# A two-layer cross-attention kernel: in the first layer's step, both halves of the weighted-value product stand together, the preparation follows them, and the second pair of search products comes last

## The chip, the cores and the metric

The kernel runs on one core of a Trainium2 chip. The metric is the device time of one execution in microseconds (us), the median of several runs. The core's engines run side by side, each through its own list of instructions in order, and wait for each other by semaphores: TensorE (PE in the profile; PEld is its weight load), VectorE (DVE), ScalarE (ACT), GpSimd (POOL) and SyncE (SP, which only issues DMAs). "Product" below means a matmul on TensorE.

## The reference

Two layers work on x (32 batches, 56 tokens, 128 channels) with a context of 1500 rows per batch. Each layer is a cross-attention and then a mixture of 8 experts. The attentions are

```python
# layer 0: 32 query-key heads of 4 channels, 16 value heads of 8; two softmaxes, their difference, an RMS norm
q, k, v = layernorm(x) @ Wq.T, ctx @ Wk.T, ctx @ Wv.T
a1 = softmax(q1 * hd**-0.5 @ k1.T) @ v;  a2 = softmax(q2 * hd**-0.5 @ k2.T) @ v
x = x + tanh(g) * (rms_norm(a1 - lam * a2) * subln_w * (1 - LAMBDA_INIT)) @ Wp.T + ...
# layer 1: 16 heads of 8 channels, a mask over the context
x = x + tanh(g) * (softmax(where(mask, -big, q @ k.T / sqrt(8))) @ v) @ Wo.T + ...
```

The change is in the attention of both layers; it matters in layer 0, which is the first half of the time.

## The kernel before

`attend` (one function for both layers) goes over the 32 batches, and in each over 12 key tiles of 125 keys: 384 *steps* a layer. The maximum of each query's scores is not found online: a *search* computes the scores of the next batch beforehand, in 48 *pieces* (112 queries by 500 keys, layer 0), four in each step, and VectorE takes the maximum of each piece. The pieces come in two pairs; the two products of a pair use different rows of TensorE. In this text **A0, A1** is the first pair of a step (`searched(n, t, 0)`) and **B0, B1** the second (`searched(n, t, 1)`). Layer 1 has only two pieces in a step, so it has no B pair.

In a step of layer 0, TensorE computes

- the *scores* of the tile (L850, two banks `score_ps`), from which ScalarE makes the exponentials `probs` (L943, two instructions);
- the pieces (L829), which VectorE reduces (L1001);
- the *weighted-value product* of the tile before (L866, fp32, `probs` times values into `acc_ps`), in two halves, `weigh(n, t - 1, 0)` and `weigh(n, t - 1, 1)`, four products each that use different columns of TensorE;
- mostly one *preparation*: a piece of work for another batch that is laid on a step by the table `where`. V is a third of the values (L803), T a third of the transposed context (L790), K a third of the keys (L798), F a transpose of the finished output (L813), A the transpose of the normalised output (L817), and M the transpose of the negated maxima (L808), which VectorE splits into two fp16 rows (L974, L976). All others are taken out of PSUM ("drained") by ScalarE.

Pieces and preparations share three PSUM banks, `spare_ps`, `max_ps0` and `max_ps1`, in strict rotation over the list `order`: whoever is at place k of that list waits until the one at place k - 3 has been drained. Before the change the places of a full step are A0 A1 B0 B1 and the preparation. So B0 waits for the preparation of the step before, B1 for A0, the preparation for A1, and the next step's A0 and A1 for B0 and B1. This is the wait:

```python
            def wait_for_room(user):

                k = place_of[user]
                if k >= len(rooms):
                    pe.wait_ge(*drained(order[k - len(rooms)]))
```

The keys of a batch go a long way: K on TensorE, ScalarE copies them out, GpSimd splits them into two fp16 parts (L720, L722), SyncE stores them to HBM (L618) and loads them into the rows of `kstack` (L628), three batches ahead. The first piece of a batch (A0 of step 7) waits for that.

Of the kernel before, what the change touches and what calls it, by code (L numbers as in the profile page):

```python
# [90 lines left out]
def at_least(eng, sem, value):  # L91

    if isinstance(value, int) and value <= 0:
        return
    eng.wait_ge(sem, value)


def build(nc, a, out):

    ctx = ExitStack()  # L100
    with ctx:
# [128 lines left out]
        feed_forward(T, 0)  # L230
        normalise(T, "norm1", 1)
        attend(T, L1)
        normalise(T, "norm1f", None, projected=1)
        feed_forward(T, 1)
# [218 lines left out]
def attend(T, L):  # L453
# [63 lines left out]

    if L is L0:
        where = {("V", 0): (0, 1), ("F", 0): (1, 1), ("F", 1): (2, 1), ("V", 1): (3, 1), ("T", 0): (4, 1), ("V", 2): (5, 1),
                 ("K", 0): (6, 1), ("M", 0): (7, 0), ("T", 1): (7, 1), ("K", 1): (8, 1), ("T", 2): (9, 1), ("K", 2): (10, 1),  # L520
                 ("A", 0): (11, 1)}
        keyed = [("T", 0), ("K", 0), ("T", 1), ("K", 1), ("T", 2), ("K", 2)]
    else:
        where = {("V", 0): (0, 1), ("F", 0): (1, 1), ("V", 1): (2, 1), ("F", 1): (3, 1), ("V", 2): (4, 1), ("K", 0): (5, 1),
                 ("K", 1): (6, 1), ("M", 0): (7, 0), ("K", 2): (8, 1), ("A", 0): (10, 1)}
        keyed = [("K", i) for i in range(NTHIRD)]
    valued = [("V", i) for i in range(NTHIRD)]
    per_step = L.pieces // NKT
# [14 lines left out]
    def at_step(n, t, side):  # L543

        return [(kind, n + LEAD[kind], i) for (kind, i), place in where.items()
                if place == (t, side) and 0 <= n + LEAD[kind] < B]

    def searched(n, t, k):


        if 2 * k >= per_step:
            return []
        d, place = (1, early + t * per_step) if t < NKT - AHEAD else (2, (t - NKT + AHEAD) * per_step)
        return [("P", n + d, place + 2 * k + r) for r in range(2)] if n + d < B else []

    order = [("P", 0, p) for p in range(L.pieces)] + [("M", 0, 0)] + [("P", 1, p) for p in range(early)]
    for n in range(B):
        for t in range(NKT):
            order += searched(n, t, 0) + at_step(n, t, 0) + searched(n, t, 1) + at_step(n, t, 1)
    order += [(kind, B - 1, i) for kind, i in turnaround]  # L560
    rooms = [spare_ps[:, :], max_ps[0][:, :], max_ps[1][:, :]]
    place_of = {user: k for k, user in enumerate(order)}
# [2 lines left out]
    def room(user):  # L565

        if user in place_of:
            return rooms[place_of[user] % len(rooms)]
        return first_banks[first_preps.index(user) % len(first_banks)]
# [9 lines left out]
    def piece(p):  # L579

        r, third, c, i = p % 2, p // 2 % NTHIRD, p // (2 * NTHIRD) % PAIRS, p // (2 * NTHIRD * PAIRS)
        return r, third, c, i, (i * 2 + r) * PAIRS + c

    with nc.Block() as block:
# [188 lines left out]
        def _(pe):  # L773
# [5 lines that stand above are left out]
# [40 lines left out]
            def search(pair):  # L819

                for _, n, p in pair:
                    if p == 0:
                        pe.wait_ge(s_ks[n % SLOTS], K_INC * (n // SLOTS + 1))
                        pe.wait_ge(s_qs, n + 1)
                for _, n, p in pair:
                    r, third, c, i, _ = piece(p)
                    rows = slice(HALF * r, HALF * r + KROWS)
                    wait_for_room(("P", n, p))
                    nc.tensor.matmul(room(("P", n, p))[0:PIECE, 0:TK], qstack[n % SLOTS][rows, c, PIECE * i:PIECE * (i + 1)],  # L829
                                     kstack[n % SLOTS][rows, c, TK * third:TK * third + TK],  # L830
                                     start=True, stop=True, skip_group_check=True).then_inc(s_piece, 1)
# [54 lines left out]
            for n in range(B):  # L886
                for t in range(NKT):
                    for h in range(H):
                        scores(n, t, h)
                    search(searched(n, t, 0))  # L890
                    for user in at_step(n, t, 0):
                        use(user)
                    for i in range(2):
                        if t:
                            weigh(n, t - 1, i)
                        elif n:
                            weigh(n - 1, LAST, i)
                        if i == 0:
                            search(searched(n, t, 1))
                    for user in at_step(n, t, 1):  # L900
                        use(user)
            for i in range(2):
                weigh(B - 1, LAST, i)
# [4 lines left out]
        @block.scalar  # L908
        def _(act):
            def drain(user):  # L910
                kind, n, i = user
                if kind == "M":
                    return
                spare_ps = room(user)
                act.wait_ge(s_ready, spare_count[user] + 1)
                if kind == "T":
                    if i == 0:
                        at_least(act, s_cst, 16 * n)
                    nc.scalar.activation(ctxT[0][:, TK * i:TK * i + TK], spare_ps[:, 0:TK], ACT.Copy).then_inc(s_ctxT, 1)
                if kind == "K":  # L920
                    at_least(act, s_kl, NTHIRD * (n - 1) + i + 1)
                    key = key_f[:, TK * i:TK * i + TK]
                    if L.masked:
                        nc.scalar.activation(key, spare_ps[:, 0:TK], ACT.Identity, bias=small["bk1"][:, :]).then_inc(s_kf, 1)
                    else:
                        nc.scalar.activation(key, spare_ps[:, 0:TK], ACT.Copy).then_inc(s_kf, 1)  # L926
                if kind == "V":
                    nc.scalar.activation(  # L928
                        vext[n % SLOTS][:, THIRD * i:THIRD * i + THIRD, :, :].rearrange("k t u (a e) -> k t (u a) e", a=2)[:, :, :, 0:VD],
                        spare_ps[0:KT, :].rearrange("k (t h d) -> k t h d", t=THIRD, d=VD), ACT.Copy).then_inc(s_v, 1)  # L930
                if kind == "F":
                    if i == 0:
                        at_least(act, s_attn, n)
                    nc.scalar.activation(turned[:, i, 0:256 * S], spare_ps[0:SQ, 0:256 * S], ACT.Copy).then_inc(s_turned, 1)
                if kind == "A":
                    nc.scalar.activation(T["attnT"][:, n * SQ:n * SQ + SQ], spare_ps[:, 0:SQ], ACT.Copy).then_inc(s_at, 1)

            def exps(n, t, h):
                number = (n * NKT + t) * H + h
                act.wait_ge(s_scores, number + 1)  # L940
                if h == 0:
                    at_least(act, s_av, n * NKT + t - 1)
                nc.scalar.activation(probs[t % 2][:, 896 * h:896 * h + 896].rearrange("k (b c) -> k b c", b=2),  # L943
                                     score_ps[(t * H + h) % 2][0:KT, :, 0:448], ACT.Exp, scale=EXP_SCALE).then_inc(s_exp, 1)

            def copy_output(n):
                act.wait_ge(s_av, n * NKT)
                nc.scalar.activation(out_sb[:, 0:L.o_cols], acc_ps[:, 0:L.o_cols], ACT.Copy).then_inc(s_os, 1)

            for user in first_preps:  # L950
                drain(user)
            for n in range(B):
                for t in range(NKT):
                    for h in range(H):
                        exps(n, t, h)
                    if t == 0 and n:
                        copy_output(n)
                    for user in at_step(n, t, 0) + at_step(n, t, 1):
                        drain(user)
            copy_output(B)  # L960
            for kind, i in turnaround:
                drain((kind, B - 1, i))
# [3 lines left out]
        def _(dve):  # L966
# [47 lines left out]
            for n in range(B):  # L1014
                for t in range(NKT):
                    for user in searched(n, t, 0):
                        reduce_piece(user)
                    for user in at_step(n, t, 0):
                        drain(user)
                    if t == where["F", 1][0] + 1 and n:  # L1020
                        reciprocals(n)
                    for user in searched(n, t, 1):
                        reduce_piece(user)
                    for user in at_step(n, t, 1):
                        drain(user)
            reciprocals(B)

# [327 lines left out]
```

## Time and profile before

| what | value |
|---|---|
| median of 3 runs (lowest, highest) | 2541.89 us (2535.67, 2550.67) |
| the profiled execution | 2538.51 us, its span on the core 2536.7 us |
| TensorE's mean granted clock | 0.952 |
| busy over the span: PE, DVE, ACT, POOL | 2371.0 us (93%), 1679.8 us (66%), 1471.6 us (58%), 1057.8 us (42%) |

The profile is of one execution. A matmul's start is recorded and its end modelled, so TensorE that shows as busy may still be waiting for a semaphore between two products; the distance from one start to the next is what tells. "PEld idle" is time in which no weights were being loaded. The loop of layer 0 lies between about 150 and 1350 us of the span, that of layer 1 between about 1590 and 2340 us.

### The profile page before, as it was taken

To read this page: it belongs to the slowest core of one execution; us is meant where nothing else is said; L and a number is where in the kernel's file an instruction comes from. 1 tells how busy PE (TensorE), PEld (TensorE's weight loads), DVE (VectorE), ACT (ScalarE), POOL (GpSimd) and SP (SyncE) were. 2 spreads that over 40 slices of the span, in tenths; PEclk is the share of its full clock that TensorE was granted. 3 is DMA by queue.
4 is the path that set the end of the run, shared out by engine and by line. 5 is a ranking of instruction groups with operands and counts; after the bars stand their busy time and mean duration, and the time that the engine had idled before them with its cause. 6 is when DMAs were issued, how large, how long until landed. Compare 5 with 4: busy or idle time off the path is not lost. (4 is left out here: it accounts for less than half of the span.)

```text
span 2536.7 us, 64926 instructions
## 1 busy us (share of the span) xinstructions
PE 2371.0 (93%) x26296; PEld 1320.2 (52%) x26296; DVE 1679.8 (66%) x3732; ACT 1471.6 (58%) x2101; POOL 1057.8 (42%) x1150
## 2 busy tenths in 40 slices
PE   4799999999999999999996976999999999999798
PEld 3244444444444444444444763566655666666576
DVE  2587777777777777777782553666666666666444
ACT  2156666666666666666675432566656666666422
POOL 4213323333333333332323347456655565663232
PEclk8589999999999999999997996899999999999799
DMA  3533434534434345343321006567665766753100
GB/s 101 104 72 76 96 95 74 112 78 91 103 78 100 91 78 109 77 96 96 74 43 49 22 28 141 107 127 135 131 121 119 123 133 126 135 130 51 51 1 14
DMA packets 157410, 227.67 MB, mean 90 GB/s; under 512 B 46052, under 2 KB 106596, under 8 KB 156612
## 3 DMA queue, kind: packets, MB, share of 16 engines
q1 hardware_dynamic: 157124, 223.67, 42.4%
q8 instruction: 202, 3.31, 0.7%
q14 instruction: 84, 0.69, 0.1%
HBM read 146.77 MB, written 76.48 MB: 88 GB/s over the span
## 5 line engine op out<-in xcount | busy, mean ns | idle before, releaser
L943 ACT ACTIVATE probs<-score_ps 125x896 f32<-125x896 f32 x1152 | 1011.4, 916 | 159.5 <-PE score_ps L850 158.6
L1001 DVE TENSOR_REDUCE max_part<-max_ps 112x1 f32<-112x500 f32 x1022 | 654.6, 670 | 177.0 <-PE spare_ps L829 87.6
L866 PE MATMUL acc_ps<-probs,vext 125*32 125x224 f32 (+1 forms) x12288 | 675.2, 315 | 3.4 <-issue 2.5
L829 PE MATMUL max_ps<-kstack,qstack 48*112 48x500 f16 x1533 | 522.1, 403 | 6.7 <-DVE max_part L1001 3.4
L1001 DVE TENSOR_REDUCE max_part<-spare_ps 112x1 f32<-112x500 f32 x514 | 344.2, 670 | 148.1 <-PE max_ps L829 147.1
L998 DVE CUSTOM_DVE_ANT_0 kstack<-max_ps,kstack 112x500 f32<-112x500 f32 x511 | 335.2, 675 | 160.2 <-PE max_ps L829 87.8
L720 POOL CAST khl<-kstack 128x500 f16<-128x500 f32 x192 | 115.0, 599 | 700.2 <-ACT kstack L926 510.2
L866 PEld LDWEIGHTS acc_ps<-probs,vext 125*32 125x32 f32 x12288 | 258.1, 108 | 262.2 <-issue 248.7
L850 PE MATMUL score_ps<-qstack,kstack 50*125 50x224 f16 (+1 forms) x6144 | 387.7, 243 | 3.3 <-ACT probs L943 1.9
L850 PEld LDWEIGHTS score_ps<-qstack,kstack 50*125 50x125 f16 x6144 | 304.5, 134 | 136.7 <-issue 95.1
L829 PE MATMUL spare_ps<-kstack,qstack 48*112 48x500 f16 x771 | 310.8, 403 | 7.0 <-DVE max_part L1001 1.9
L829 PEld LDWEIGHTS max_ps<-kstack,qstack 48*112 48x112 f16 x1533 | 170.2, 128 | 186.4 <-DVE max_part L1001 87.3
L737 POOL TENSOR_TENSOR heads_out<-turned,rden 56x64 f32<-56x64 f32 x192 | 55.3, 288 | 481.4 <-DVE rden L984 471.4
L998 DVE CUSTOM_DVE_ANT_0 kstack<-spare_ps,kstack 112x500 f32<-112x500 f32 x257 | 173.6, 675 | 122.9 <-PE max_ps L829 114.9
L722 POOL TENSOR_TENSOR khl<-kstack,khl 128x500 f16<-128x500 f32 x192 | 204.9, 1067 | 15.4
L1309 POOL TENSOR_TENSOR kstack<-kstack,probs 112x512 f32 (+1 forms) x68 | 90.6, 1332 | 171.6 <-DVE probs L1256 171.6
L844 PE MATMUL score_ps<-kstack 56*125 56x448 f16 x768 | 157.9, 401 | 2.1 <-issue 2.1
L829 PEld LDWEIGHTS spare_ps<-kstack,qstack 48*112 48x112 f16 x771 | 98.7, 128 | 100.9 <-DVE max_part L1001 45.5
L928 ACT ACTIVATE vext<-max_ps 125x512 f32<-125x512 f32 x117 | 69.9, 597 | 117.5 <-PE max_ps L803 117.5
L803 PE MATMUL max_ps<-wide,ctx_f 128*125 128x128 f32 x936 | 135.9, 289 | 1.3 <-issue 1.3
L803 PEld LDWEIGHTS max_ps<-wide,ctx_f 128*125 128x125 f32 x936 | 113.2, 190 | 32.6 <-issue 17.8
L711 POOL TENSOR_SCALAR kstack<-mask_in 112x1500 bf16<-112x1500 uint8 x32 | 127.8, 3993 | 2.6
(184 smaller groups left out, 2613.3 us busy)
## 6 DMA issues: line engine op xcount, KB each, us to landing
kstack<-k_parts SPq DMA_DIRECT2D x384, 187.5 KB, 6.6
k_parts<-khl SPq DMA_DIRECT2D x128, 375.0 KB, 5.5
ctx_f<-in_ctx SPq DMA_DIRECT2D x32, 750.0 KB
context_parts<-ctx_f SPq DMA_DIRECT2D x32, 750.0 KB, 4.7
ctx_f<-context_parts SPq DMA_DIRECT2D x32, 750.0 KB, 4.3
mask_in<-in_mask SPq DMA_DIRECT2D x128, 82.0 KB
qrows<-q_parts SPq DMA_DIRECT2D x384, 7.0 KB, 7.4
qstack<-max_rows SPq DMA_DIRECT2D x384, 0.9 KB
```

Of the source, the lines that this page charges most:

```text
L711: nc.gpsimd.tensor_scalar(mask_add[n % SLOTS], T["mask_in2"][:, :], -BIG * BIG, None, ALU.mult).then_inc(s_add, 1)
L720: nc.gpsimd.tensor_copy(khl[:, 0, k], key_f[:, k]).then_inc(s_kh, 1)
L722: nc.gpsimd.tensor_tensor(khl[:, 1, k], key_f[:, k], khl[:, 0, k], ALU.subtract).then_inc(s_kl, 1)
L803: last = nc.tensor.matmul(spare_ps[0:KT, D * t:D * t + D], ctxT[n % len(ctxT)][:, c:c + KT], Wv[:, :], start=True, stop=True)
L829: nc.tensor.matmul(room(("P", n, p))[0:PIECE, 0:TK], qstack[n % SLOTS][rows, c, PIECE * i:PIECE * (i + 1)], kstack[n % SLOTS][rows, c, TK ...
L844: nc.tensor.matmul(buf[0:KT, r, 0:448], mask_f[n % SLOTS][HALF * r:HALF * r + SQ, keys], big_eye[HALF * r:HALF * r + SQ, :], start=True, s ...
L850: last = nc.tensor.matmul(buf[0:KT, r, GC * k:GC * (k + 1)], kstack[n % SLOTS][rows, h * here + k, keys], qstack[n % SLOTS][rows, h * here ...
L866: last = nc.tensor.matmul(acc_ps[32 * j:32 * j + 32, TT * S * i:TT * S * (i + 1)].rearrange("p (s c) -> p s c", s=S), vext[n % SLOTS][:, t ...
L943: nc.scalar.activation(probs[t % 2][:, 896 * h:896 * h + 896].rearrange("k (b c) -> k b c", b=2), score_ps[(t * H + h) % 2][0:KT, :, 0:448 ...
L998: nc.vector.tensor_tensor_reduce(masked_scores[p % 2], scores, mask_add[n % SLOTS][:, TK * third:TK * third + TK], 1.0, -3.0e38, ALU.add, ...
L1001: nc.vector.reduce_max(best, scores, AX.X).then_inc(s_red, 1)
L1309: nc.gpsimd.tensor_tensor(k, k, tmp[e % DB][:, :, :], ALU.add).then_inc(s_acc, 1)
```

## The change

In each step the second half of the weighted-value product moves ahead of the B pair, and so does the preparation: the step becomes scores, A0 A1, both halves of the weighted-value product, the preparation, B0 B1. There is a third place in a step, 2, behind the B pair. In the table of layer 0, M gets a step of its own (7), the preparations from T1 on go one step later, and A follows the B pair of step 11. In layer 1 all preparations have place 2, which is where they were, but for M, which goes from before the weighted-value product to behind it. The list `order` follows, so the rotation of the banks becomes A0 A1 preparation B0 B1.

```diff
@@ -517,12 +517,12 @@
     if L is L0:
         where = {("V", 0): (0, 1), ("F", 0): (1, 1), ("F", 1): (2, 1), ("V", 1): (3, 1), ("T", 0): (4, 1), ("V", 2): (5, 1),
-                 ("K", 0): (6, 1), ("M", 0): (7, 0), ("T", 1): (7, 1), ("K", 1): (8, 1), ("T", 2): (9, 1), ("K", 2): (10, 1),
-                 ("A", 0): (11, 1)}
+                 ("K", 0): (6, 1), ("M", 0): (7, 1), ("T", 1): (8, 1), ("K", 1): (9, 1), ("T", 2): (10, 1), ("K", 2): (11, 1),
+                 ("A", 0): (11, 2)}
...
@@ -556,7 +556,7 @@
-            order += searched(n, t, 0) + at_step(n, t, 0) + searched(n, t, 1) + at_step(n, t, 1)
+            order += searched(n, t, 0) + at_step(n, t, 1) + searched(n, t, 1) + at_step(n, t, 2)
...
@@ -888,16 +888,15 @@
                     search(searched(n, t, 0))
-                    for user in at_step(n, t, 0):
-                        use(user)
                     for i in range(2):
                         if t:
                             weigh(n, t - 1, i)
                         elif n:
                             weigh(n - 1, LAST, i)
-                        if i == 0:
-                            search(searched(n, t, 1))
                     for user in at_step(n, t, 1):
+                        use(user)
+                    search(searched(n, t, 1))
+                    for user in at_step(n, t, 2):
                         use(user)
```

ScalarE and VectorE drain in the same new order; their own instructions are the same.

How the programs stand on TensorE, at three places. First an ordinary step of layer 0, with V as its preparation; the names are the banks. Before:

```order
L850 MATMUL score_ps0<-qstack0,kstack0 125x224 x4
L850 MATMUL score_ps1<-qstack0,kstack0 125x224 x4
L829 MATMUL spare_ps<-kstack1,qstack1 112x500
L829 MATMUL max_ps0<-kstack1,qstack1 112x500
L866 MATMUL acc_ps<-probs0,vext0 32x224 x4
L829 MATMUL max_ps1<-kstack1,qstack1 112x500
L829 MATMUL spare_ps<-kstack1,qstack1 112x500
L866 MATMUL acc_ps<-probs0,vext0 32x224 x4
L803 MATMUL max_ps0<-wide,ctx_f 125x128 x4
```

After, from the B pair of the step before to this step's B pair:

```order
L829 MATMUL max_ps1<-kstack2,qstack2 112x500
L829 MATMUL spare_ps<-kstack2,qstack2 112x500
L850 MATMUL score_ps0<-qstack1,kstack1 125x224 x4
L850 MATMUL score_ps1<-qstack1,kstack1 125x224 x4
L829 MATMUL max_ps0<-kstack2,qstack2 112x500
L829 MATMUL max_ps1<-kstack2,qstack2 112x500
L866 MATMUL acc_ps<-probs0,vext1 32x224 x8
L803 MATMUL spare_ps<-wide,ctx_f 125x128 x4
L829 MATMUL max_ps0<-kstack2,qstack2 112x500
L829 MATMUL max_ps1<-kstack2,qstack2 112x500
```

Before, B1 uses the bank of A0 (`spare_ps`), with half of the weighted-value product between them. After, B0 and B1 use the banks of A0 and A1, and it is A1 that uses the bank of the B0 just before it (`max_ps1`), with the scores between them.

Second, step 7 of layer 0 with M (L808). Before:

```order
L829 MATMUL max_ps1<-kstack2,qstack2 112x500
L829 MATMUL spare_ps<-kstack2,qstack2 112x500
L808 MATMUL max_ps0<-wide,neg_max 16x112
L866 MATMUL acc_ps<-probs0,vext0 32x224 x4
L829 MATMUL max_ps1<-kstack2,qstack2 112x500
L829 MATMUL spare_ps<-kstack2,qstack2 112x500
L866 MATMUL acc_ps<-probs0,vext0 32x224 x4
L790 MATMUL max_ps0<-wide,ctx_f 128x125 x4
```

After, with the A pair of step 8:

```order
L829 MATMUL spare_ps<-kstack0,qstack0 112x500
L829 MATMUL max_ps0<-kstack0,qstack0 112x500
L866 MATMUL acc_ps<-probs0,vext1 32x224 x8
L808 MATMUL max_ps1<-wide,neg_max 16x112
L829 MATMUL spare_ps<-kstack0,qstack0 112x500
L829 MATMUL max_ps0<-kstack0,qstack0 112x500
L850 MATMUL score_ps0<-qstack1,kstack1 125x224 x4
L850 MATMUL score_ps1<-qstack1,kstack1 125x224 x4
L829 MATMUL max_ps1<-kstack0,qstack0 112x500
L829 MATMUL spare_ps<-kstack0,qstack0 112x500
```

M has moved behind the weighted-value product and is the only preparation of its step.

Third, from the end of a batch (step 11) into step 0 of the next. Before:

```order
L829 MATMUL max_ps0<-kstack2,qstack2 112x500
L829 MATMUL max_ps1<-kstack2,qstack2 112x500
L866 MATMUL acc_ps<-probs0,vext0 32x224 x4
L817 MATMUL spare_ps<-wide,attn_n 128x56
L850 MATMUL score_ps0<-qstack1,kstack1 125x224 x4
L850 MATMUL score_ps1<-qstack1,kstack1 125x224 x4
L829 MATMUL max_ps0<-kstack2,qstack2 112x500
L829 MATMUL max_ps1<-kstack2,qstack2 112x500
```

After:

```order
L798 MATMUL spare_ps<-ctx_f,wk_order 128x500
L829 MATMUL max_ps0<-kstack2,qstack2 112x500
L829 MATMUL max_ps1<-kstack2,qstack2 112x500
L817 MATMUL spare_ps<-wide,attn_n 128x56
L850 MATMUL score_ps0<-qstack1,kstack1 125x224 x4
L850 MATMUL score_ps1<-qstack1,kstack1 125x224 x4
L829 MATMUL max_ps0<-kstack2,qstack2 112x500
L829 MATMUL max_ps1<-kstack2,qstack2 112x500
L866 MATMUL acc_ps<-probs1,vext0 32x224 x8
```

Step 11 now has K2 (L798) as well as A (L817). A's bank is that of K2, and both products of the next A pair use the banks of the B pair.

## Rows read from the trace of the kernel before

**Rows 1.** Layer 0's loop: length, busy PE, PEld, DVE, ACT, POOL; clock; DMA share; GB/s.
```profile
150.00:1290.00 1140.00, 1130.97 (x11278) 529.12 (x11271) 876.35 (x1541) 777.05 (x1075) 389.59 (x579) 1.00 0.43 90
```

**Rows 2.** Timeline of PE, step 6: start, us taken, instruction.
```profile
625.01 0.60 PE L850 MATMUL score_ps<-qstack,kstack 50*125 50x224 f16 x8
625.44 0.37 PE L829 MATMUL spare_ps<-kstack,qstack 48*112 48x500 f16 x1
625.45 0.37 PE L829 MATMUL max_ps<-kstack,qstack 48*112 48x500 f16 x1
625.75 0.59 PE L866 MATMUL acc_ps<-probs,vext 125*32 125x224 f32 x8
626.26 0.41 PE L829 MATMUL max_ps<-kstack,qstack 48*112 48x500 f16 x1
626.59 0.41 PE L829 MATMUL spare_ps<-kstack,qstack 48*112 48x500 f16 x1
626.93 0.59 PE L866 MATMUL acc_ps<-probs,vext 125*32 125x224 f32 x8
627.45 1.10 PE L798 MATMUL max_ps<-ctx_f,wk_order 128*128 128x500 f32 x2
628.48 0.60 PE L850 MATMUL score_ps<-qstack,kstack 50*125 50x224 f16 x8
```

**Rows 3.** Timeline of DVE, steps 6 and 7 of the same batch.
```profile
625.85 0.68 DVE L1001 TENSOR_REDUCE max_part<-spare_ps 112x1 f32<-112x500 f32 x1 [1.07 <-PE max_ps L829]
626.45 1.25 DVE L1001 TENSOR_REDUCE max_part<-max_ps 112x1 f32<-112x500 f32 x2
...
628.32 0.20 DVE L1004 TENSOR_REDUCE neg_max<-max_part 112x16 f32<-112x48 f32 x1
...
630.58 0.25 DVE L974 TENSOR_SCALAR max_rows<-max_ps 16x112 f16<-16x112 f32 x1
```

**Rows 4.** Timeline of PE, the end of layer 0's loop, where there are no pieces.
```profile
1330.45 0.96 PE L866 MATMUL acc_ps<-probs,vext 125*32 125x224 f32 x16
1331.34 0.80 PE L850 MATMUL score_ps<-qstack,kstack 50*125 50x224 f16 x8
```

**Rows 5.** Timeline of PE, one B pair that starts together behind an fp32 product.
```profile
1235.03 0.41 PE L829 MATMUL spare_ps<-kstack,qstack 48*112 48x500 f16 x1
```

**Rows 6.** Timeline of DVE, the reduction of that pair's first piece.
```profile
1235.48 0.68 DVE L1001 TENSOR_REDUCE max_part<-spare_ps 112x1 f32<-112x500 f32 x1
```

**Rows 7.** Timeline of PE, step 7 with M.
```profile
629.23 0.26 PE L808 MATMUL max_ps<-wide,neg_max 112*16 112x112 f32 x1
...
631.58 0.65 PE L790 MATMUL max_ps<-wide,ctx_f 125*128 125x125 f32 x4
632.15 0.60 PE L850 MATMUL score_ps<-qstack,kstack 50*125 50x224 f16 x8
```

**Rows 8.** Timeline of PE, step 0 of the next batch.
```profile
644.57 0.65 PE L850 MATMUL score_ps<-qstack,kstack 50*125 50x224 f16 x8
...
647.18 1.14 PE L803 MATMUL max_ps<-wide,ctx_f 128*125 128x128 f32 x8
648.25 0.60 PE L850 MATMUL score_ps<-qstack,kstack 50*125 50x224 f16 x8
```

**Rows 9.** Timeline of ACT, the drain of step 6's preparation K.
```profile
628.59 0.59 ACT L926 ACTIVATE kstack<-max_ps 128x500 f32<-128x500 f32 x1 [1.26 <-PE max_ps L798]
```

**Rows 10.** Timeline of PE, the scores of step 11, and M one batch later.
```profile
642.12 0.60 PE L850 MATMUL score_ps<-qstack,kstack 50*125 50x224 f16 x8
...
668.49 0.26 PE L808 MATMUL max_ps<-wide,neg_max 112*16 112x112 f32 x1
```

**Rows 11.** Timeline of SP, one batch's keys stored, then loaded; DMA issues.
```profile
643.51 6.52 SPq L618 DMA_DIRECT2D k_parts<-khl  x2
654.17 2.67 SPq L628 DMA_DIRECT2D kstack<-k_parts  x6
```

**Rows 12.** The six loads of L628 from 654 to 657 us, by source line.
```profile
DMA to landing us min/median/max: 3.8/6.7/9.4
```

More of the change, by code:

```diff
@@ L519, in attend @@
         where = {("V", 0): (0, 1), ("F", 0): (1, 1), ("F", 1): (2, 1), ("V", 1): (3, 1), ("T", 0): (4, 1), ("V", 2): (5, 1),
-                 ("K", 0): (6, 1), ("M", 0): (7, 0), ("T", 1): (7, 1), ("K", 1): (8, 1), ("T", 2): (9, 1), ("K", 2): (10, 1),
-                 ("A", 0): (11, 1)}
+                 ("K", 0): (6, 1), ("M", 0): (7, 1), ("T", 1): (8, 1), ("K", 1): (9, 1), ("T", 2): (10, 1), ("K", 2): (11, 1),
+                 ("A", 0): (11, 2)}
         keyed = [("T", 0), ("K", 0), ("T", 1), ("K", 1), ("T", 2), ("K", 2)]
     else:
-        where = {("V", 0): (0, 1), ("F", 0): (1, 1), ("V", 1): (2, 1), ("F", 1): (3, 1), ("V", 2): (4, 1), ("K", 0): (5, 1),
-                 ("K", 1): (6, 1), ("M", 0): (7, 0), ("K", 2): (8, 1), ("A", 0): (10, 1)}
+        where = {("V", 0): (0, 2), ("F", 0): (1, 2), ("V", 1): (2, 2), ("F", 1): (3, 2), ("V", 2): (4, 2), ("K", 0): (5, 2),
+                 ("K", 1): (6, 2), ("M", 0): (7, 2), ("K", 2): (8, 2), ("A", 0): (10, 2)}
         keyed = [("K", i) for i in range(NTHIRD)]
@@ L957, in _ @@
                         copy_output(n)
-                    for user in at_step(n, t, 0) + at_step(n, t, 1):
+                    for user in at_step(n, t, 1) + at_step(n, t, 2):
                         drain(user)
@@ L1017, in _ @@
                         reduce_piece(user)
-                    for user in at_step(n, t, 0):
+                    for user in at_step(n, t, 1):
                         drain(user)
@@ L1023, in _ @@
                         reduce_piece(user)
-                    for user in at_step(n, t, 1):
+                    for user in at_step(n, t, 2):
                         drain(user)
```

## The prediction

> **What bounds the kernel now.** I read the busy times of layer 0's loop first, then the timeline of TensorE step by step, then VectorE's and ScalarE's beside it. In the loop TensorE shows as busy for 1131.0 of 1140 us, VectorE for 876.4, ScalarE for 777.1, at the full clock [rows 1]. So the order on TensorE decides, but busy is not working: what counts is the distance between starts.
>
> Step 6 goes from 625.01 to 628.48 [rows 2]. Its parts, start to start: scores 0.43, the A pair 0.31 (both products start at once), half a weighted-value product 0.51, B0 0.33, B1 0.34, the other half 0.52, the preparation K 1.03. The two B products don't start together. VectorE starts to reduce A0 0.41 after the A pair's start and takes 0.68, until 626.53 [rows 3]; B1, which uses A0's bank, starts at 626.59, 0.06 later [rows 2]. So a chain runs through the step: A pair, 0.41, reduction 0.68, 0.06, B1, then 0.34 to the second half. That is 1.49 from the pair's start to the second half's start, and the first half of the product and B0 lie inside it for nothing. A step is 0.43 + 1.49 + 0.52 = 2.44, plus its preparation. The other preparations cost about 1.07 for V [rows 8] and 0.57 for T [rows 7]; F is like T.
>
> Two places are dearer. Step 7, with M and T1, takes 3.67 from 628.48 to 632.15 [rows 2, 7], which is 0.66 over 2.44 + 0.57. Step 0 takes 3.68, which is 0.17 over 2.44 + 1.07 [rows 8]: its A pair has to wait for both products of the last B pair, since A took a place between them. One batch takes 668.49 - 629.23 = 39.26 us from M to M [rows 7, 10]. The parts agree: 12 x 2.44 + 0.66 + 0.17, and three V, three K and five T or F (9.15), are 39.26. So A, in step 11, costs nothing of its own.
>
> **The change, an ordinary step.** The instructions are the same; only their order and the rotation move. B0 and B1 now wait for A0 and A1 of the same step, and the whole weighted-value product and a preparation lie between: they will start together. But A1 now waits for the B0 just before it, with only the scores in between. So the chain is not gone, it starts at the B pair:
>
> - from the B pair to the start of B0's reduction: 0.45. This pair stands behind an fp32 preparation; the pair of the old kernel that starts together behind an fp32 product has 1235.03 to 1235.48 [rows 5, 6]. If it is like the pair behind the scores, it is 0.41 [rows 2, 3].
> - the reduction 0.68 and the release 0.06, as above. A1 then starts alone 1.19 after the B pair. The B products (at most 0.31) and the scores 0.43 are hidden under this; A0 also waits until ScalarE has drained the preparation. That drain starts 628.59 - 627.45 = 1.14 after the product K and takes 0.59 [rows 2, 9], so it ends 1.14 + 0.59 - 1.03 = 0.70 after the B pair: hidden too, with 0.4 to spare.
> - A1 to the weighted-value product: 0.34, as B1 has it now. Behind the waiting A1 stand only the product and the preparation; ScalarE already has the scores and isn't held up.
> - both halves in one piece: 0.89 [rows 4], against 0.51 + 0.52.
> - the preparation, as before.
>
> That makes 0.45 + 0.68 + 0.06 + 0.34 + 0.89 = 2.42 plus the preparation, against 2.44. What was won at B is paid at A1: before, half a product (0.51) hid in the chain, and now the scores (0.43) do. The joined product gives 0.14 back, the worse cover takes 0.08, the later start of the reduction 0.04: **0.02 less a step**. VectorE keeps up: its reductions start 0.60 apart [rows 3], so four started at 0.45 end at 0.45 + 3 x 0.60 + 0.68 = 2.93, before the next B pair even in a step with T (2.99). The bound at 0.41 makes it 0.06 less a step; if the joined product gave nothing, 0.12 more.
>
> At the joined product a rule bears on this. By the Trainium skill (TensorEngine Tiling (Array Packing), Key Properties) changing the tiling mode drains TensorE. This case's trace agrees that a seam costs something, 0.14 where it can be seen both ways; by the rule a step goes from five changes of mode to three, and at 0.14 each the sum would be 2.28 plus the preparation. I keep 2.42. The same page (Performance Considerations) warns that packing does not speed up the emptying of PSUM, which may become the bottleneck. That speaks against this change, and it is what the chain through the reduction shows.
>
> **M's step.** M is now alone in step 7, behind the product. Taking the B pair of step 6 as 0: its reductions start at 0.45 and 1.05; neg_max (0.20 [rows 3]) waits for the end of the second, so A0's starts at about 1.95 and A1's at 2.55. M is issued at 2.42 and waits for nothing, but its own drain comes third on VectorE: at 3.15, two instructions of 0.25 [rows 3], and only then B0's reduction, 3.65 to 4.33. A1 of step 8 can start at 4.39, its product at 4.73. In an ordinary step the product would start at 1.53, so M's step takes 3.20, with no preparation besides.
>
> **A, between two batches.** A now uses K2's bank in the same step, so it waits for ScalarE's drain, until 0.76 after the B pair. The scores follow, and A1 of step 0 needs the bank of B1, not B0: B1's reduction starts at 1.05, ends at 1.73, A1 at 1.79. That is 0.60 more than 1.19.
>
> **The sum for a batch.** The eleven preparations V, K, T, F are the same. Before: 12 x 2.44 + 0.66 + 0.17 = 30.11. After: 11 x 2.42 + 3.20 + 0.60 = 30.42. So a batch gets 0.31 longer, over some 29 batches that have all of it, **+9 us**. At the end of the loop, where T and K are missing, M no longer stands in front of the product waiting for the maxima: perhaps 1 us less. In layer 1 only M moves, from before the product to behind it, in the same place of the rotation; it costs or gives some hundredth of a microsecond to a tenth, once a batch: 0 to -2. I take -2 for both. The profiled execution becomes 2538.5 + 7 = 2545.5 us. It lies 3.4 below the median of its three runs, so I put the median at **2547**.
>
> **What else could happen.** About 0.5% (13 us) is what a measurement of this kernel can tell from no change.
>
> *The gain comes through.* If A1 didn't wait, because the rotation or VectorE were quicker than I read it, B would cost 0.31 instead of 0.67 and the product 0.89 instead of 1.03: 0.50 less in each of some 350 steps, 175 us, 2365 us. For it speaks that the B pair really does start together; against it the bank names, by which A1 follows B0. Chance 0.04.
>
> *A second seam saved.* TensorE changes between the kinds of product five times in a step now and three times after. The joined product shows one seam, 0.14 [rows 2, 4]. If the chain got a second 0.14 shorter, a step would be 0.16 cheaper than now; eleven times that, less the 0.53 more at M and A (3.20 + 0.60 - 2.44 - 0.66 - 0.17), is 1.2 us a batch, 36 us, 2506; with half of the seam 2529. Against it: a second seam that goes lies between B and the scores, under the chain. Chance 0.08. This is what the rule of the Trainium skill's page TensorEngine Tiling (Array Packing) would give at full size.
>
> *The keys come too late (slower).* K2 is now in step 11, not 10, and A0 of step 7 needs the keys in `kstack`. In the profile the store is issued at 643.51, the last load at about 656.4, and the slowest landing takes 9.4: 665.8 [rows 11, 12], and A0 comes at 668.18, if M stands 0.31 behind the pair as the product does in rows 2 [rows 2, 10]. So 2.4 us are to spare. From the end of K2 to A0 of step 7 it is now 668.18 - 642.12 = 26.06 us [rows 10]; after, one A step and six others plus 0.76: 4.09 + 5.98 + 3.49 + 2.99 + 3.49 + 3.45 + 0.76 = 24.25, 1.8 less. Then 0.6 us are left in this batch. If the loads land 1.6 us later than now, because they meet the context loads otherwise, each batch waits 1 us: 29 us, 2575. It decides from 0.6 us of delay on. SyncE's queue keeps its order: the stores of the context go one step later too, and M's rows, some 0.8 us later, aren't needed before the next batch's scores. Chance 0.12.
>
> *The hand-overs cost double (slower).* The stalls at M and A are put together from single rows; if M's step takes 0.5 more, by waits one behind the other on VectorE, and A's 0.3, it is 0.8 a batch, 23 us: 2570. Also an ordinary step dearer by 0.06 does it. Chance 0.16.
>
> *As forecast*, 2547, own range 2535 to 2558, chance 0.60.
>
> **The numbers.** Faster than 2529 are the gain that comes through and most of the seams: 0.11. Slower than 2555 are most of the two slower cases and the forecast's upper edge: 0.29. Between, 0.60. For the range I leave out the gain that comes through, the lower end of the seams and the far end of the late keys: 2526 to 2573.
>
> **What would show it.** In the profile after: the B pair starts together and A1 alone, about 1.19 behind the B pair, 0.06 after the end of B0's reduction; the joined product takes 0.89; a step with K about 3.45 from B pair to B pair; step 7 about 3.2; the A pair of step 0 more than half a microsecond apart. A batch, M to M, 39.6 us. I am wrong if A0 and A1 start together, if A0 of step 7 waits for a DMA, or if a batch comes out below 38.9 or above 39.9.

## The result, and the profile after

| | before | after |
|---|---|---|
| median of 20 runs each (lowest, highest) | 2540.24 us (2535.15, 2551.51) | 2548.73 us (2540.47, 2558.53) |
| ratio, 95% interval | | 1.0030 (1.0019 to 1.0040) |
| the profiled execution, its span | 2538.51, 2536.7 | 2546.45, 2544.7 |

The changed kernel is 0.3% slower, 8.5 us, inside what the prediction called no difference (0.5%); with 20 runs of each the interval leaves out 1, so the 0.3% are small but there. That a change that rearranges every step of layer 0 moves so little is the thing to explain. In what follows, the line numbers behind the changed lines (from L890 on) are one lower than before: L925 is ScalarE's copy of a K, L942 the exponentials, L1000 the reduction of a piece, L1003 the negated maxima, L973 and L975 M's drain.

The loop of layer 0 first, with the columns of [rows 1] (length, then busy time and number of instructions of PE, PEld, DVE, ACT and POOL, then clock, DMA share, GB/s):

```profile
150.00:1290.00 1140.00, 1109.73 (x11168) 576.62 (x11166) 867.10 (x1525) 792.23 (x1065) 385.50 (x567) 1.00 0.42 89
```

TensorE shows 21 us less busy time and finishes 110 instructions fewer in the same 1140 us: 1% less work is done in the same time. Then the timeline of TensorE over one step with K, the counterpart of [rows 2]:

```profile
601.99 0.41 PE L829 MATMUL spare_ps<-kstack,qstack 48*112 48x500 f16 x1
601.99 0.41 PE L829 MATMUL max_ps<-kstack,qstack 48*112 48x500 f16 x1
602.24 0.55 PE L850 MATMUL score_ps<-qstack,kstack 50*125 50x224 f16 x8
602.74 0.41 PE L829 MATMUL max_ps<-kstack,qstack 48*112 48x500 f16 x1
603.17 0.41 PE L829 MATMUL spare_ps<-kstack,qstack 48*112 48x500 f16 x1
603.52 0.96 PE L866 MATMUL acc_ps<-probs,vext 125*32 125x224 f32 x16
604.41 1.11 PE L798 MATMUL max_ps<-ctx_f,wk_order 128*128 128x500 f32 x2
605.45 0.41 PE L829 MATMUL max_ps<-kstack,qstack 48*112 48x500 f16 x1
```

The B pair starts together at 601.99. A0 comes at 602.74, but A1 only at 603.17, 1.18 behind the B pair, and the product at 603.52, 1.53 behind it. The stall has moved from B1 to A1. From B pair to B pair the step takes 3.46; the old step 6 takes 3.47 [rows 2]. TensorE is shown as busy almost throughout, since A0's modelled duration (0.41 from 602.74) covers the wait.

M's step, on TensorE, against [rows 7]:

```profile
635.40 0.41 PE L829 MATMUL max_ps<-kstack,qstack 48*112 48x500 f16 x1
...
636.58 0.41 PE L829 MATMUL spare_ps<-kstack,qstack 48*112 48x500 f16 x1
636.92 0.96 PE L866 MATMUL acc_ps<-probs,vext 125*32 125x224 f32 x16
637.82 0.26 PE L808 MATMUL max_ps<-wide,neg_max 112*16 112x112 f32 x1
638.12 0.41 PE L829 MATMUL max_ps<-kstack,qstack 48*112 48x500 f16 x1
638.70 0.41 PE L829 MATMUL spare_ps<-kstack,qstack 48*112 48x500 f16 x1 [0.17 <-DVE max_part L1000]
...
639.75 0.41 PE L829 MATMUL max_ps<-kstack,qstack 48*112 48x500 f16 x1 [0.17 <-DVE max_part L1000]
640.10 0.40 PE L866 MATMUL acc_ps<-probs,vext 125*32 125x224 f32 x4
```

and on VectorE:

```profile
637.38 0.68 DVE L1000 TENSOR_REDUCE max_part<-max_ps 112x1 f32<-112x500 f32 x1
...
638.57 0.25 DVE L973 TENSOR_SCALAR max_rows<-max_ps 16x112 f16<-16x112 f32 x1
...
639.04 0.66 DVE L1000 TENSOR_REDUCE max_part<-max_ps 112x1 f32<-112x500 f32 x1
```

M's drain stands behind two reductions and in front of B0's, which starts at 639.04; A1 follows at 639.75. From product (636.92) to product (640.10) M's step takes 3.18. In this batch it is the one step whose B pair doesn't start together: B1 (638.70) waits for A1's reduction, since only the product and the short M lie between. It delays nothing, for the next A1 waits until later still, for B0's.

The end of a batch on TensorE, against [rows 8], and ScalarE's drain of K2:

```profile
611.92 0.41 PE L829 MATMUL max_ps<-kstack,qstack 48*112 48x500 f16 x1
612.66 0.26 PE L817 MATMUL max_ps<-wide,attn_n 56*128 56x56 f32 x1 [0.33 <-ACT kstack L925]
...
613.68 0.41 PE L829 MATMUL max_ps<-kstack,qstack 48*112 48x500 f16 x1
614.03 0.40 PE L866 MATMUL acc_ps<-probs,vext 125*32 125x224 f32 x4
```
```profile
612.02 0.59 ACT L925 ACTIVATE kstack<-max_ps 128x500 f32<-128x500 f32 x1 [1.19 <-PE max_ps L798]
```

A (L817) waits for the drain. The product of the next step (614.03) comes 2.11 behind the B pair (611.92) instead of 1.53, for A1 (613.68) now has to wait for B1's reduction. The next M is here, so that a batch takes 677.41 - 637.82 = 39.59 us, against 39.26 [rows 7, 10]:

```profile
677.41 0.27 PE L808 MATMUL max_ps<-wide,neg_max 112*16 112x112 f32 x1
```

### The profile page after: what moved, and what is told of

The parts are those of the page before. It is cut to its first block and busy times, and to the rows that moved or that the text cites. A ratio compares the mean times of both kernels' runs of the same rounds, so it can differ in the third digit from the quotient of the medians.

```text
span 2544.7 us, 64926 instructions
## 1 busy us (share of the span) xinstructions
PE 2355.8 (93%) x26296; PEld 1372.5 (54%) x26296; DVE 1678.8 (66%) x3732; ACT 1494.7 (59%) x2101; POOL 1058.9 (42%) x1150
## 5 line engine op out<-in xcount | busy, mean ns | idle before, releaser
L942 ACT ACTIVATE probs<-score_ps 125x896 f32<-125x896 f32 x1152 | 1013.7, 915 | 203.1 <-PE score_ps L850 201.5
L1000 DVE TENSOR_REDUCE max_part<-max_ps 112x1 f32<-112x500 f32 x1023 | 654.1, 669 | 191.3 <-PE max_ps L829 95.3
L866 PE MATMUL acc_ps<-probs,vext 125*32 125x224 f32 (+1 forms) x12288 | 601.3, 313 | 2.4 <-issue 1.5
L829 PE MATMUL max_ps<-kstack,qstack 48*112 48x500 f16 x1534 | 551.1, 416 | 16.1 <-DVE max_part L1000 7.8
L1000 DVE TENSOR_REDUCE max_part<-spare_ps 112x1 f32<-112x500 f32 x513 | 343.4, 669 | 147.7 <-PE max_ps L829 147.3
L866 PEld LDWEIGHTS acc_ps<-probs,vext 125*32 125x32 f32 x12288 | 296.1, 109 | 217.2 <-issue 165.5
L850 PE MATMUL score_ps<-qstack,kstack 50*125 50x224 f16 (+1 forms) x6144 | 377.5, 238 | 2.9 <-ACT probs L942 1.9
L850 PEld LDWEIGHTS score_ps<-qstack,kstack 50*125 50x125 f16 x6144 | 336.2, 134 | 53.0 <-ACT probs L942 7.1
L829 PE MATMUL spare_ps<-kstack,qstack 48*112 48x500 f16 x770 | 319.8, 415 | 12.1 <-DVE max_part L1000 4.6
```

Source lines behind the costliest of these rows:

```text
L850: last = nc.tensor.matmul(buf[0:KT, r, GC * k:GC * (k + 1)], kstack[n % SLOTS][rows, h * here + k, keys], qstack[n % SLOTS][rows, h * here ...
L866: last = nc.tensor.matmul(acc_ps[32 * j:32 * j + 32, TT * S * i:TT * S * (i + 1)].rearrange("p (s c) -> p s c", s=S), vext[n % SLOTS][:, t ...
L1000: nc.vector.reduce_max(best, scores, AX.X).then_inc(s_red, 1)
```

## The experiments

All are timed against the kernel before, run beside them on the same chip. "A batch" is the distance from one M to the next in the steady part of layer 0.

**1. Only the joined product.** The kernel before with this edit alone; table and rotation stay:

```diff
                         elif n:
                             weigh(n - 1, LAST, i)
-                        if i == 0:
-                            search(searched(n, t, 1))
+                    search(searched(n, t, 1))
```

> The kernel before with one part of the change alone: both halves of the weighted-value product together, then the B pair, then the preparation; the table and the rotation A0 A1 B0 B1 preparation stay. Theory (a chain through VectorE's reduction and the three banks sets the step): B1 waits for A0's reduction, which ends 1.15 us after the A pair; the joined product (0.31 + 0.89 = 1.20) covers that, so B0 and B1 start together. The preparation then waits for A1's reduction, 1.75 after the A pair (0.41 + 0.60 + 0.68 + 0.06). A step with V or K is 0.43 + 1.75 + preparation = 3.21 to 3.25 instead of 3.47 to 3.51, one with T or F about 2.8 instead of 3.0. Some 2.6 us less a batch, 75 us less in all, about 2465. Rival (only the seam between the kinds of product counts, the pair stays one by one): 0.14 less a step, about 2490. Rival (TensorE's own work bounds the loop): no change.

Measured: 2468.53 us (4 runs), ratio 0.972 (0.969 to 0.974), a batch 36.90. This is 70 us below the kernel before and 80 below the changed one, of which it is a part. The timeline of TensorE, a step with T:

```profile
628.21 0.37 PE L829 MATMUL spare_ps<-kstack,qstack 48*112 48x500 f16 x1
628.22 0.37 PE L829 MATMUL max_ps<-kstack,qstack 48*112 48x500 f16 x1
628.52 0.96 PE L866 MATMUL acc_ps<-probs,vext 125*32 125x224 f32 x16
629.41 0.41 PE L829 MATMUL max_ps<-kstack,qstack 48*112 48x500 f16 x1
629.42 0.41 PE L829 MATMUL spare_ps<-kstack,qstack 48*112 48x500 f16 x1
629.94 0.65 PE L790 MATMUL max_ps<-wide,ctx_f 125*128 125x125 f32 x4
```

Both pairs start together. B1 still uses A0's bank, and that wait of 1.15 us (0.41 to the reduction, 0.68, 0.06) is now covered by the A pair and the whole product, 1.20. The preparation uses A1's bank and starts 1.73 behind the A pair, as the same sum with the second reduction says (0.41 + 0.60 + 0.68 + 0.06 = 1.75). So the join is the good part of the change. What loses 80 us is the other part: the preparation ahead of the B pair, with the rotation and the table that go with it.

**2. The cover put back.** The changed kernel, with the second half of the product behind the B pair. ScalarE also drains step 0's preparation before it copies the output, so that the next A0, which uses that preparation's bank, doesn't wait for the copy. This second edit touches one step of twelve and was not run alone.

```diff
                     for i in range(2):
                         if t:
                             weigh(n, t - 1, i)
                         elif n:
                             weigh(n - 1, LAST, i)
-                    for user in at_step(n, t, 1):
-                        use(user)
-                    search(searched(n, t, 1))
+                        if i == 0:
+                            for user in at_step(n, t, 1):
+                                use(user)
+                            search(searched(n, t, 1))
```

> The kernel after, with the second half of the weighted-value product moved behind the B pair (scores, A0 A1, half the product, preparation, B0 B1, the other half); ScalarE drains the preparation of step 0 before it copies the output. The rotation is that of after. Theory: A1 waits for B0's reduction, 1.19 after the B pair; now 0.34 + 0.52 + 0.43 = 1.29 lie between, so A0 and A1 start together, and the step is 1.29 + 0.31 + 0.51 = 2.11 plus the preparation, if the next B1 need not wait for A1's reduction (3.03 after the B pair): 3.14 with K, 3.18 with V instead of 3.45 and 3.49; with T or F that wait makes it about 3.03, as now. Some 2 us less a batch, 55 us less than after, about 2490. Rival (the two seams more cost 0.14 each and nothing was waiting): 50 to 100 us more than after, about 2600.

Measured: 2498.45 us (4 runs), ratio 0.984 (0.982 to 0.987), a batch 37.97 (39.59 in the changed kernel): 50 us faster than the changed kernel, with more changes of product kind, not fewer. TensorE in a step with T:

```profile
602.82 0.37 PE L829 MATMUL max_ps<-kstack,qstack 48*112 48x500 f16 x1
...
603.13 0.59 PE L866 MATMUL acc_ps<-probs,vext 125*32 125x224 f32 x8
603.64 0.65 PE L790 MATMUL max_ps<-wide,ctx_f 125*128 125x125 f32 x4
604.22 0.41 PE L829 MATMUL max_ps<-kstack,qstack 48*112 48x500 f16 x1
604.55 0.42 PE L829 MATMUL spare_ps<-kstack,qstack 48*112 48x500 f16 x1
```

With half a product and the scores between the B pair and the next A pair, the A pair starts together. In this step the B pair doesn't: B1 (604.55) waits for A1's reduction, 1.72 behind A1, and the short T is not cover enough. That keeps T's step at 3.03 (602.82 to 605.85), where the changed kernel has 3.00. The gain is in the steps with V and K: in the same trace they take 3.19 (599.63 to 602.82) and 3.15 (609.04 to 612.19), where the changed kernel needs 3.49 (628.44 to 631.93) and 3.46.

**3. Half a reduction, in the changed kernel and in the one before.** VectorE reduces only the first 250 of 500 columns in layer 0, so part of each maximum is left out.

```diff
-                    nc.vector.reduce_max(best, scores, AX.X).then_inc(s_red, 1)
+                    nc.vector.reduce_max(best, scores[:, 0:TK // 2], AX.X).then_inc(s_red, 1)
```

In the changed kernel:

> The kernel after, in which VectorE reduces only the first 250 of the 500 columns of each piece in layer 0; the maxima miss the other half. TensorE's work and order are untouched. Theory: the reduction (0.68) is a link of each step's chain from B0 to A1; at about 0.42 it shortens a step by 0.26, M's step and A's hand-over by more: about 3.5 to 4 us a batch, 2430 to 2445. Rival (TensorE is bound by its own work, the waits are covered): within 10 us of after.

Measured: 2430.14 us (4 runs), at the lower end of what was expected, ratio 0.958 (0.955 to 0.960), a batch 35.8 to 37.0. VectorE's reduction behind a B pair that starts at 600.45:

```profile
600.90 0.42 DVE L1000 TENSOR_REDUCE max_part<-max_ps 112x1 f32<-112x250 f32 x1 [1.22 <-PE spare_ps L829]
```

It takes 0.42 instead of 0.68, and the product starts at 601.72, 1.27 behind the pair instead of 1.53: TensorE gets all of VectorE's 0.26 back. In the kernel before:

> The kernel before, with VectorE reducing only the first 250 of a piece's 500 columns in layer 0 (so part of each maximum is left out). It asks whether the order before hangs on the reduction as the changed one does. If it does, B1 is released some 0.28 us earlier in each step, until it meets the end of the first half of the product: a batch takes about 3.4 us less than its 39.25, 35.9, and the time is 2435 (2425 to 2450), as much under the kernel before as the same edit brought the changed kernel. If the order before had hung on TensorE's own work, as rival, it would stay within 15 us of the kernel before.

Measured: 2422.79 us (2 runs), ratio 0.954 (0.950 to 0.958), a batch 35.73: just below the expected 2425 to 2450, for the search ahead of the loop got 13 us shorter as well (the loop's first scores come at 120.58 instead of 133.77), which I had not counted. Both orders hang on the same chain, through the reduction, and to the same degree: 3.5 us a batch here, about 3.4 there.

**4. Layer 1's part alone.** The kernel before with `("M", 0): (7, 1)` in the table of layer 1.

> The kernel before, with the change in layer 1 alone: M behind the weighted-value product. Layer 0 is as before. Theory: M has the same place in the rotation and nobody waits longer, so no difference beyond 2 us; the 5 us by which layer 1 was shorter in the profile of after come from a few uneven batches that both profiles have. Rival: moving M is worth 5 us, about 2535.

Measured: 2536.83 us (13 runs), ratio 0.9997 (0.9981 to 1.0013). It makes no difference that can be measured; anything from 5 us less to 3 us more stays possible, and so the rival of 5 us less is not excluded.

**5. A ahead of K2.** The changed kernel, with one place in the table moved:

```diff
-("T", 2): (10, 1), ("K", 2): (11, 1), ("A", 0): (11, 2)}
+("T", 2): (10, 1), ("A", 0): (11, 1), ("K", 2): (11, 1)}
```

> The changed kernel with A in step 11 ahead of K2, both before the B pair, instead of behind it. The rotation then runs B0 B1 A0 A1 at the batch's end with nothing between, so A1 of step 0 waits for B0 and not for B1. If the 0.59 us that the hand-over costs come from A's place in the rotation, as I say, about 0.45 of them go (A's own 0.1 is then paid): a batch 39.15 instead of 39.58, the kernel 13 us faster than the changed one, about 2534 against 2547, some 0.998 of the kernel before. Rival: the wait at the boundary is due to the copy of the output or to the end of the batch on ScalarE; then it stays within 3 us of the changed kernel, 1.003.

Measured: 2533.92 us (12 runs), ratio 0.998 (0.996 to 1.000), a batch 39.20. The end of a batch on TensorE:

```profile
644.60 0.27 PE L817 MATMUL spare_ps<-wide,attn_n 56*128 56x56 f32 x1
644.79 1.10 PE L798 MATMUL max_ps<-ctx_f,wk_order 128*128 128x500 f32 x2
...
646.57 0.85 PE L829 MATMUL max_ps<-kstack,qstack 48*112 48x500 f16 x2
647.36 0.96 PE L866 MATMUL acc_ps<-probs,vext 125*32 125x224 f32 x16
```

The product comes 1.53 behind the B pair (645.83), as in any step. The 0.58 were the place of A in the rotation; A ahead of K2 costs 0.19 of its own (644.60 to 644.79), and the difference is what a batch gets shorter, 39.59 to 39.20.

**6. The late clock.** In the trace after, the start of layer 0's loop is some 3 us longer than the steady excess and M's later place in its step explain. The first M in the loop comes 40.32 us behind the M of the search ahead, before 35.83; 1.3 of the difference are M's place, which was 0.3 and is now 1.6 behind its step's A pair. TensorE's granted clock stays at the lower level (0.50, 1.2 GHz) until 151 us, before until 140. This is the window 144 to 150 us; the granted clock is the third number from the right. Before:

```profile
144.00:150.00 6.00, 6.00 (x72) 3.02 (x64) 4.92 (x9) 3.92 (x5) 0.00 (x0) 1.00 0.01 3
```

After:

```profile
144.00:150.00 6.00, 6.00 (x48) 3.15 (x41) 3.27 (x6) 2.23 (x3) 0.00 (x0) 0.50 0.01 3
```

The next kernel is the changed one, but batch 0 of layer 0 has the order, the table and the rotation of the kernel before:

```diff
+                    if L is L0 and n == 0:
+                        for user in at_step(n, t, 0):
+                            use(user)
+                        for i in range(2):
+                            if t:
+                                weigh(n, t - 1, i)
+                            if i == 0:
+                                search(searched(n, t, 1))
+                        for user in at_step(n, t, 1):
+                            use(user)
+                        continue
```

> The changed kernel, but batch 0 of layer 0 stands in the order and rotation of the kernel before. It asks what the late rise of TensorE's clock belongs to: in the trace of before the first stretch at half clock ends at 140.5 us, in that of the changed kernel at 151.1, and its first batch takes 3.2 us longer. If this hangs on the order of batch 0, the stretch ends at 138 to 143 us again, and the kernel is 3 us faster than the changed one, 2544, ratio about 1.002. Rival: it is chance from execution to execution, or hangs on the later batches: then the stretch may end anywhere between 127 and 152, and the time is that of the changed kernel, 2547, ratio 1.003.

Measured: 2546.62 us (12 runs), ratio 1.0027 (1.0008 to 1.0045), an interval that holds both expected ratios, 1.002 and 1.003, so that the time decides nothing. The same window does:

```profile
144.00:150.00 6.00, 6.00 (x48) 2.04 (x41) 4.53 (x8) 2.36 (x3) 0.00 (x0) 0.53 0.01 3
```

The theory fell: with the old order in batch 0 the clock rises at about 150 all the same. Until 140 its products come in the order and at the distances of the kernel before, 0.22 us earlier. The two kernels were then profiled once more each.

> The kernel before, unchanged, for one more profile. It asks how much the end of TensorE's first stretch at half clock moves with the same instructions. The kernel with batch 0 in the order before kept the half clock until about 150 us, although its instructions up to there are those of the kernel before, whose trace has 140.5: so I now expect an end anywhere between 138 and 152 us. The steady batch must be 39.25 and the one time within 2528 to 2555. Rival: the end belongs to the order after all and the kernel with batch 0 in the order before was an exception; then it is 139 to 143 here and 149 to 152 for the changed kernel.

> The changed kernel, unchanged, for one more profile. As for the kernel before: an end of the first stretch at half clock anywhere between 138 and 152 us if it is chance, 149 to 152 if it belongs to the changed order. The steady batch must be 39.58 and the one time within 2537 to 2560.

One run each: 2535.75 and 2542.80 us (the kernel before once more beside them: 2544.32), a batch 39.25 and 39.59. The window 144 to 150, before and after:

```profile
144.00:150.00 6.00, 6.00 (x65) 3.01 (x64) 4.92 (x9) 3.85 (x6) 0.00 (x0) 1.00 0.01 3
```
```profile
144.00:150.00 6.00, 6.00 (x47) 2.64 (x47) 3.98 (x7) 2.95 (x4) 0.00 (x0) 0.50 0.01 3
```

So each of the two programs does nearly the same again: the rise is at 140.5 and 141.0 before, at 151.1 and 151.8 after. But the order doesn't tell where it is. The kernel of experiment 4, whose layer 0 is that of the kernel before, rises at 142.8, and this one with batch 0 as before at 149.8. Of the kernels with the changed rotation, that of experiment 5 shows a clock of 0.85 in this window and rises at about 145, and that of experiment 2 has risen before 140. What sets it stays open.

**7. The preparation first.** The changed kernel with the preparation between scores and A pair, so that the join keeps its cover and the rotation is A0 A1 B0 B1 preparation again. M is between product and B pair of step 7, T1 and the later ones have the steps of the kernel before, V1 comes ahead of F0 and F1, and ScalarE drains step 0's preparation before it copies the output.

```diff
                     for h in range(H):
                         scores(n, t, h)
+                    for user in at_step(n, t, 0):
+                        use(user)
                     search(searched(n, t, 0))
```

> A step with both halves of the product together, as in the change, but with the preparation in front of the A pair: scores, preparation, A0 A1, both halves, B0 B1. M stands between product and B pair of step 7, and T1 and the rest keep the steps they have before; ScalarE drains step 0's preparation before it copies the output. By the chains (a piece's bank is free 1.15 us after its pair's start for the first, 1.75 for the second) the product covers B1's wait for A0 (0.31 + 0.89 = 1.20), and scores plus a V or K cover A1's wait for B1 (0.31 + 0.43 + 1.05 = 1.79). A step with V or K is then 2.99, one with T, F or A 2.98, M adds 0.3 to 0.7: a batch 36.2 to 36.6, the time 2453 (2440 to 2465), below the version that has only the joined product (2468.5, a batch 36.90). Rival: the waits for ScalarE's drain (B0 waits for the preparation) take over at steps with K and V; then a step of these costs 3.2 or more, a batch 37.5 or more, and the time lies above 2480.

Measured: 2458.58 us (4 runs), ratio 0.969 (0.966 to 0.972), a batch 36.54. It beats both kernels and the joined product alone. TensorE, a step with T and one with K:

```profile
602.00 0.41 PE L829 MATMUL spare_ps<-kstack,qstack 48*112 48x500 f16 x1
...
602.73 0.65 PE L790 MATMUL max_ps<-wide,ctx_f 125*128 125x125 f32 x4
603.31 0.42 PE L829 MATMUL max_ps<-kstack,qstack 48*112 48x500 f16 x1
603.77 0.41 PE L829 MATMUL spare_ps<-kstack,qstack 48*112 48x500 f16 x1
...
605.01 0.42 PE L829 MATMUL max_ps<-kstack,qstack 48*112 48x500 f16 x2
...
606.78 0.42 PE L829 MATMUL max_ps<-kstack,qstack 48*112 48x500 f16 x2
...
608.02 0.41 PE L829 MATMUL spare_ps<-kstack,qstack 48*112 48x500 f16 x1
```

The step with K (605.01 to 608.02) has no stall and the one with T (602.00 to 605.01) waits 0.46 for B1's reduction, until 1.77 behind the B pair. Both take 3.01, expected were 2.99 and 2.98.

## Why the prediction was right

Time (2547 against 2548.7) and mechanism hold; that the time is so close is partly luck. By its steps:

- *The chain is not gone, it starts at the B pair.* Shown by the bank names, by A1 at 1.18 (predicted 1.19), and by experiments 1 to 3: put more work between a piece and the next user of its bank, or shorten the reduction, and time falls by as much as the chain says.
- *An ordinary step.* Product 1.53 behind the B pair, both halves in 0.89 (603.52 to 604.41), step with K 3.46, as predicted about 3.45. The 0.02 that each of eleven steps should save are too small for a single step's rows to show.
- *M's step*: 3.20 predicted, 3.18 measured, with B0's reduction at 3.64 behind the B pair of the step before (3.65).
- *A, between two batches*: +0.60 predicted; 0.58 of it seen, and experiment 5 takes it away by A's place alone.
- *The sum for a batch*: +0.31 predicted, +0.33 measured, over 29 batches 9 to 10 us. This is the part that the prediction got right for the right reason.
- *-2 for the loop's end and layer 1*: not resolved. Experiment 4 leaves 5 us less to 3 us more for layer 1's part.
- *The clock at the loop's start*: some +3 us, in no step of the prediction. Experiment 6 shows that batch 0's order doesn't set it.

From its first scores to its last product layer 0's loop takes 1223.5 and 1223.8 us in the two profiles of the kernel before, 1235.8 and 1236.0 in those of the changed one: 12 us more, where the sum had 8 to 9. Layer 1's loop, measured alike, takes 762.2 and 756.1 before, 757.0 and 752.1 after. It is 4 or 5 us shorter after, but two executions of the same program differ in it by 6 and by 5. The 8 us between the first two profiles are thus 12 in layer 0's loop, 5 less in layer 1's and 1 more elsewhere. Whether moving M in layer 1 gives some of those 5 stays open: apart from experiment 4, the profiles with M moved there have 752 to 758 us in layer 1's loop and those without 756 to 769, but experiment 4's own profile, of its slowest run, has 783. The missed 3 us and the 5 less cancel in part, and that is the luck.

The rivals. *The gain comes through* (2365) and *a second seam saved* (2506) didn't happen. The rule in the Trainium skill (TensorEngine Tiling (Array Packing), Key Properties) that a change of tiling mode drains TensorE did not decide: experiment 2 has two seams more than the changed kernel and is 50 us faster. What decided is what the same page of the Trainium skill (Performance Considerations) warns of, that packing speeds up TensorE and not the emptying of PSUM, which may become the bottleneck. This trace agrees: a bank was taken again 1.15 us after its piece started before the change and 1.18 after it, and 0.68 of that is the reduction. *The keys come too late* (2575): K2 in step 11 leaves less room, but enough. In the batch of the rows above, the loads of the keys by source line:

```profile
L628 SPq DMA_DIRECT2D kstack<-k_parts x6: 319/426/434, 623.7 to 625.9; - x6
DMA to landing us min/median/max: 3.7/6.9/8.6
```

The last is issued at 625.9 and the slowest takes 8.6, so all are there by 634.5, and A0 of step 7 starts at 636.24. 1.7 us are left, and no wait of TensorE for a DMA stands in the view of waits of this loop (below). The prediction had put 0.6 us. Its way from the end of K2 to A0 was right (24.25, here 636.24 - 611.91 = 24.33), but the keys came sooner: here the slowest load takes 8.6 where it took 9.4. *The hand-overs cost double* (2570): they cost what single rows said, 3.18 and 0.58.

What the prediction did not see is its own first term. It priced the change as one piece and found the join worth 0.14 a step. The join was worth 2.35 us a batch as long as the rotation stayed, since A pair and product together are 1.20, just over the 1.15 that B1 waits for. The same change also moved the rotation and spent it again.

## What to carry to other kernels

With a rotation of few banks, find for each user who had its bank before, and add up the work between the two: it has to be longer than the way through PSUM's emptying, here 1.15 us for a pair's first piece and 1.75 for its second. An order that puts the long products into the short gaps gains; one that opens one gap by closing another gains nothing. And split a change that moves two things: here one part gave 70 us and the other took 80. Experiment 7 shows the use of it: with the join kept and the preparation where it covers most of A1's wait for B1, a batch is 36.54.

## What the runs showed of the hardware

TensorE's busy share hides a wait between two products. The view of waits over layer 0's loop of the changed kernel:

```profile
PE max_ps L829 <- DVE max_part L1000: 6.5, 38, 0.2
PE max_ps L817 <- ACT kstack L925: 6.3, 19, 0.3
PE spare_ps L829 <- DVE max_part L1000: 3.4, 20, 0.2
PE spare_ps L817 <- ACT kstack L925: 3.0, 9, 0.3
```

It lists 9.9 us of waits for VectorE, 58 times, while the halved reduction gives 118 us back: 13 ahead of the loop (its first scores at 120.89 instead of 134.27), the rest in it, which is 107 us shorter. Only start-to-start distances showed the stall.

TensorE's granted clock rose from 0.50 to 1.00 (1.2 to 2.4 GHz) near the loop's start, while the engine showed as busy without a pause (6.00 of 6 us in the windows of experiment 6), at 140 us in the kernel before and at 151 in the changed one, and within 1 us of that in a second execution of each. It is worth some 3 us here, a third of the whole difference of 8.5. Where a program rises can't be read from its order: with layer 0 as before it was 142.8 in experiment 4's kernel, with batch 0 as before 150 in experiment 6's, with A ahead of K2 145.
